# A gated SmoothQuant and mixture-of-experts layer on one core: work moved between VectorE, ScalarE and GpSimd, and the engines' orders rewritten

## The reference

```python
def smooth_quant_linear(x, w):            # x: [T, D], w: [O, D]
    s = sqrt(max(amax_x, 1e-6) / max(amax_w, 1e-6))    # per feature: maxima of |x|, |w| over rows
    xs, ws = x / s, w * s
    x_scale, w_scale = rowmax(|xs|) / 127, rowmax(|ws|) / 127
    return round(xs / x_scale) @ round(ws / w_scale).T * x_scale * w_scale.T

def xattn(x, gu, dw):                     # one batch: gate and up weights, down weights
    gate, up = split(smooth_quant_linear(x, gu))
    return smooth_quant_linear(silu(gate) * up, dw)

def ffn(x):                               # 1024 tokens, 8 experts, room for 128 tokens each
    gates = softmax(x @ w_gate); e = argmax(gates)     # top 1, first come first served
    return gates[e] * (gelu(x @ w1[e]) @ w2[e])        # tokens past an expert's room: 0

x = x + tanh(g_xattn) * xattn(layernorm(x), ctx_gu, ctx_d)
x = x + tanh(g_ffn) * ffn(layernorm(x))
```

## Time and profile before

| | before |
|---|---|
| time of the runs shown | 108.6 us, median of 3 (108.21 to 108.82) |
| profiled execution, device time | 108.64 us |
| its span, first to last instruction | 106.8 us |
| busy share of the span: PE, DVE, ACT, POOL | 90%, 78%, 67%, 55% |
| granted TensorE clock, mean | 0.998 |
| HBM read, written | 20.46 MB, 2.10 MB |

### The profile page before, as it was taken

How to read it: one execution, slowest core, us unless ns; L and a number is a source line. 1 busy time by engine, 2 the same in 40 slices (tenths; PEclk the granted TensorE clock), 3 DMA queues, 4 the chain that set the end, 5 groups by cost and what they waited for, 6 DMA issues and landing times.

```text
span 106.8 us, 2202 instructions
## 1 busy us (share of the span) xinstructions
PE 96.1 (90%) x740; PEld 81.5 (76%) x740; DVE 83.6 (78%) x243; ACT 71.7 (67%) x158; POOL 58.2 (55%) x102
## 2 busy tenths in 40 slices
PE   0999599998799999999999999999999999999940
PEld 0336358877656977889789998999989999899930
DVE  1599999999892999999795299999959669397510
ACT  5012999999899899619842919997849748396000
POOL 6063779898988589967777103452705207051141
PEclk9999999999999999999999999999999999999999
DMA  0999199989962932401586999997999200001011
GB/s 27 278 301 354 56 392 371 372 272 412 302 219 58 333 109 96 167 33 29 134 368 218 396 357 407 352 421 219 403 392 364 72 0 34 15 0 55 0 49 49
DMA packets 14602, 22.66 MB, mean 212 GB/s; under 512 B 1287, under 2 KB 13063, under 8 KB 13568
## 3 DMA queue, kind: packets, MB, share of 16 engines
q1 hardware_dynamic: 13824, 20.46, 55.1%
q0 software_dynamic: 768, 2.07, 5.4%
HBM read 20.46 MB, written 2.10 MB: 211 GB/s over the span
## 4 chain that ended last, share of the span: by engine, by line
PE 59%; DVE 27%; POOL 5%; issue 4%; POOLq 1%; DVEq 0%
PE bk L1425 27%; PE bk L1436 12%; PE bk L1438 6%; PE bk L1244 6%; DVE am L805 4%; DVE x L886 3%; DVE am L758 2%; PE bk L1372 2%; PE bk L1409 2%; DVE wide_a L826 2%; DVE am L752 2%; POOL wide_a L376 1%; POOLq L38 1%; DVE prio L901 1%; DVE ama L853 1%
## 5 line engine op out<-in xcount | busy, mean ns | idle before, releaser
L498 POOL DMA_INDIRECT out<-xrow,sidx x8 | 14.1, 1758 | 31.3 <-DVE xrow L1050 29.8
L1425 PE MATMUL bk<-rows_w,w_sb 128*128 128x128 f32 x192 | 23.1, 276 | 0.1
L1425 PEld LDWEIGHTS bk<-rows_w,w_sb 128*128 128x128 f32 x192 | 22.2, 192 | 0.3 <-DVE rows_w L992 0.2
L1436 PE MATMUL bk<-w2p,hh 128*128 128x512 f32 x56 | 20.7, 408 | 0.1
L1038 DVE TENSOR_TENSOR hl<-bk,hh 128x512 fp32r<-128x512 f32 x16 | 10.8, 686 | 6.8 <-ACT hh L611 6.7
L1438 PE MATMUL bk<-w2p,hl 128*128 128x256 f32 x56 | 15.7, 281 | 0.0
L590 ACT ACTIVATE w2p<-w_sb 128x1024 fp32r<-128x1024 f32 x12 | 12.3, 1054 | 5.0 <-PE bk L1438 5.0
L1244 PE MATMUL bk<-identb,upper 128*128 128x512 bf16 x40 | 12.3, 450 | 2.6 <-POOL upper L311 2.6
L1031 DVE TENSOR_TENSOR w2p<-w_sb,w2p 128x1024 fp32r<-128x1024 f32 x12 | 14.2, 1218 | 0.3
L1436 PEld LDWEIGHTS bk<-w2p,hh 128*128 128x128 f32 x56 | 10.6, 189 | 2.8 <-issue 0.6
L604 ACT ACTIVATE bk<-bk 128x512 f32<-128x512 f32 x16 | 9.4, 585 | 2.0 <-PE bk L1425 2.0
(11 more groups left out here) (177 smaller groups left out, 225.2 us busy)
## 6 DMA issues: line engine op xcount, KB each, us to landing
w_sb<-in_w SPq DMA_DIRECT2D x12, 1024.0 KB, 6.6
x<-in_x SPq DMA_DIRECT2D x4, 256.0 KB, 3.9
cw<-in_ctx_gu SPq DMA_DIRECT2D x4, 256.0 KB, 4.4
cw<-in_w SPq DMA_DIRECT2D x1, 1024.0 KB, 5.7
out<-x SPq DMA_DIRECT2D x4, 256.0 KB, 2.5
x<-in_w SPq DMA_DIRECT2D x1, 1024.0 KB, 4.9
wide_a<-in_w SPq DMA_DIRECT2D x1, 1024.0 KB, 4.9
wide_b<-in_w SPq DMA_DIRECT2D x1, 1024.0 KB, 8.4
```

Source lines behind the costliest of these rows:

```text
L498: nc.gpsimd.indirect_dma_start(out_rows, bass.IndirectOffsetOnAxis(ap=sidx[:, e:e + 1], axis=0), yo[:, e % 2, :], None, bounds_check=last_ ...
L1425: ins = nc.tensor.matmul(HB[e % 2][:, m, n * C:(n + 1) * C], wv[:, k, f:f + P], xgT[:, e % B, k], start=(k == 0), stop=(k == K - 1))
L1436: nc.tensor.matmul(YB[e % 2], hh[:, e % 2, n], w2p[:, e % 2, n].rearrange("p a d -> p (a d)"), start=(n == 0), stop=False)
```

## The change

The arithmetic is the same; two formulas are written with fewer operations, some operations change their engine, and the lists are written in another order.

- `floor_w` goes: the guard is taken inside `product_w` and `ratio1`. `mean_eps` leaves VectorE and becomes a third operation of GpSimd's `row_part`.
- The gate and up weights of batch 3 are scaled by GpSimd (`scale1_w(3)`) instead of ScalarE; `load_w2(3)` and `turn2(3, 1)` wait for that.
- The down weights are scaled by VectorE (`scale_dw`) instead of ScalarE; `turn4` waits for both.
- The second norm's six rows on GpSimd and two on VectorE become four on ScalarE (`norm2(0)`, `norm2(1)`, with a new `shift2` on GpSimd), three on GpSimd and one on VectorE.
- `split_low` and `expert_out` can do part of their range. `split_low(0, 1)` runs in two halves, one of them right behind `add_x(0)`; `expert_out(0, 1)` in four parts, with `slots_turn(1)` in their middle. Two of the fills go.
- ScalarE's `split_high(0, 0)` and `(0, 1)` move ahead to `scale2`, the tanh of the gates to the first `quantise1`. The load of the gelu table stays behind `half_logits`.

```diff
-            sp.wait_ge(scaled1[1], B)
+            sp.wait_ge(scaled1[1], B - 1)
+            sp.wait_ge(scaled_pool, 1)
             load_w2(3)
...
+            def scale1_w(b):
+
+                pool.wait_ge(scale1_ready, b + 1)
+                for k in range(K):
+                    last = nc.gpsimd.tensor_scalar(xs1[:, b, K + k], cw[:, b, k], sc1[:, b, K + k:K + k + 1], 1.0, ALU.mult,
+                                                   ALU.mult)
+                last.then_inc(scaled_pool, 1)
...
                 link(nc.gpsimd.tensor_tensor(std1[:, b], ve1[:, b], rs1[:, b], ALU.mult))
+                nc.gpsimd.tensor_scalar(x[:, b, :, D], nm1[:, b], -1.0, DELTA, ALU.mult, ALU.add)
...
+            def shift2(b):
+
+                pool.wait_ge(rstd2_ready, b + 1)
+                nc.gpsimd.tensor_tensor(sh2[:, b], nm2[:, b], x1[:, b, :, D + L], ALU.mult).then_inc(shift2_ready, 1)
...
-                nc.scalar.activation(aw[:, b, 0], a_sb[:, b], ACT.Identity, scale=sc3[:, b, 0:1])
-                nc.scalar.activation(aw[:, b, 1], dw[:, b], ACT.Identity,
-                                     scale=sc3[:, b, 1:2]).then_inc(scaled2, 1)
+                nc.scalar.activation(aw[:, b, 0], a_sb[:, b], ACT.Identity, scale=sc3[:, b, 0:1]).then_inc(scaled2, 1)
...
+            def norm2(b):
+
+                act.wait_ge(shift2_ready, b + 1)
+                for j in range(J):
+                    last = nc.scalar.activation(xn2[:, b, j], x1[:, b, j, 0:D], ACT.Identity, scale=x1[:, b, j, D + L:H],
+                                                bias=sh2[:, b, j:j + 1])
+                last.then_inc(norm2_act_ready, 1)
...
-                done["product_w", b] = mark(nc.vector.tensor_tensor(pr1[:, b], am1[:, b, 0:K], rw1[:, b], ALU.mult))
+                done["product_w", b] = mark(nc.vector.scalar_tensor_tensor(
+                    out=pr1[:, b], in0=am1[:, b, 0:K], scalar=EPS, in1=rw1[:, b], op0=ALU.max, op1=ALU.mult))
...
-                nc.vector.tensor_tensor(ra1[:, b], pr1[:, b], fl1[:, b], ALU.max).then_inc(ratio1_ready, 1)
+                nc.vector.tensor_scalar(ra1[:, b], pr1[:, b], EPS * EPS, None, ALU.max).then_inc(ratio1_ready, 1)
...
+            def scale_dw(b):
+
+                dve.wait_ge(scale2_ready, b + 1)
+                nc.vector.tensor_scalar(aw[:, b, 1], dw[:, b], sc3[:, b, 1:2], None, ALU.mult).then_inc(scaled_dw, 1)
...
-            def split_low(e, h):
+            def split_low(e, h, first=0, count=4):
...
+                part = slice(4 * h + first, 4 * h + first + count)
...
+                pe.wait_ge(scaled_dw, b + 1)
...
-            def expert_out(e, m):
+            def expert_out(e, m, first=0, count=4):
...
-            fill(2, 0, 2)
             expert_out(0, 0)
+            expert_out(0, 1, 0, 1)
+            expert_out(0, 1, 1, 1)
             slots_turn(1)
-            expert_out(0, 1)
+            expert_out(0, 1, 2, 1)
+            expert_out(0, 1, 3, 1)
```

More of the change, by code:

```diff
@@ L634, in _ @@
             quantise1(0, 1)
+            quantise1(0, 0)
+            tanh_gates()
             scale1(2, 0)
-            quantise1(0, 0)
+            quantise1(1, 1)
             quantise1(1, 0)
-            quantise1(1, 1)
+            move1(0)
+            quantise1(2, 1)
+            scale1(3, 0)
             move_row1(0)
[L640 to L643, removed]
+            move_row1(1)
             quantise1(2, 0)
-            move_row1(1)
+            move1(1)
+            quantise1(3, 1)
             silu(0)
-            quantise1(3, 1)
-            move1(1)
+            quantise1(3, 0)
             move1(2)
-            quantise1(3, 0)
+            silu(1)
             move_row1(2)
-            silu(1)
+            move_row1(3)
+            move1(3)
             silu(2)
             scale2(0)
-            move1(3)
-            move_row1(3)
+            split_high(0, 0)
+            silu(3)
             scale2(1)
-            silu(3)
+            split_high(0, 1)
             quantise2(0)
             scale2(2)
-            tanh_gates()
+            scale2(3)
             quantise2(1)
-            scale2(3)
             move2(0)
-            move2(1)
             quantise2(2)
             quantise2(3)
+            move2(1)
+            move2(2)
             square2(0)
-            move2(2)
             square2(1)
+            square2(2)
             move2(3)
-            split_high(0, 0)
-            square2(2)
+            norm2(0)
+            norm2(1)
             square2(3)
             first_turned()
-            split_high(0, 1)
+            split_high(1, 0)
             half_logits()
@@ L883, in add_x @@
                 dve.wait_ge(row_x_ready, b + 1)
-                dve.wait_ge(dve_c, max(done["mean_eps", b], done["minus_mean", b]))
+                dve.wait_ge(dve_c, done["minus_mean", b])
                 for j in range(J):
@@ L1163, in _ @@
             amax4(3)
-            mean_eps(3)
             guard4(3)
@@ L1204, in _ @@
             hotc_(3)
+            relative_logits()
             first_turned()
+            ovr()
             gather_index()
             scatter_index()
[L1208 removed]
             split_low(0, 0)
[L1210 to L1211 removed]
+            split_low(0, 1, 2, 2)
+            split_low(1, 0)
             hidden_low(0, 0)
@@ L1216, in _ @@
             expert_in(2)
+            expert_in(3)
             softmax()
-            expert_in(3)
+            slot_gates_out()
             hidden_low(1, 0)
-            split_low(1, 0)
+            hidden_low(1, 1)
             split_low(1, 1)
-            slot_gates_out()
-            hidden_low(1, 1)
             expert_add(0)
@@ L1434, in expert_out @@
                     pe.wait_ge(y_ready, e - 1)
-                for n in range(4 * m, 4 * m + 4):
+                for n in range(4 * m + first, 4 * m + first + count):
                     nc.tensor.matmul(YB[e % 2], hh[:, e % 2, n], w2p[:, e % 2, n].rearrange("p a d -> p (a d)"),
@@ L1439, in expert_out @@
                                            start=False, stop=(n == NF - 1))
-                if m == 1:
+                if m == 1 and first + count == 4:
                     ins.then_inc(y_used, 1)
@@ L1498, in _ @@
             fill(1, 1, 6)
+            turn4(2)
             turn5(0)
+            turn4(3)
             fill(2, 1, 3)
-            turn4(2)
+            product2(0)
             turn5(1)
-            turn4(3)
-            product2(0)
+            turn5(2)
             product2(1)
-            turn5(2)
+            product2(2)
+            positions(0)
             fill(3, 1, 1)
             turn5(3)
-            positions(0)
             positions(1)
-            product2(2)
             product2(3)
+            positions(2)
             sort(0)
             sort(1)
-            index(0)
-            positions(2)
             positions(3)
             sort(2)
+            index(0)
             sort(3)
```

217 lines of the change are left out of this document (107 added, 110 removed).

## The result

The changed kernel took 113.79 us (median of 4 runs, 112.44 to 114.07), the kernel before 108.53 us beside it: a ratio of 1.0444, with a 95% interval of 1.0405 to 1.0483. It is slower by 5.3 us, where 108.4 us was forecast and the range ended at 109.3 us. The profiled execution took 113.73 us with a span of 111.8 us, so its span is 5.0 us longer than before.

The account below looks back on a forecast made before the run. TensorE bounds the kernel from 48.05 us, mostly VectorE before. Span 106.8 - 0.04 (earlier start) - 0.15 (after it) = 106.6 us; with 1.84 us around it 108.45 us, forecast 108.4 us, range 107.3 to 109.3 us.

Parts of the forecast that it names:

- ScalarE, GpSimd and VectorE up to add_x(0): Before the residual additions: silu(1) 1.13 us earlier, second act product 1.21 earlier, recip4(1) 0.62 later, add_x(0) 1.29 earlier.
- second rival: VectorE and GpSimd hinder each other, scale_dw at 0.50 us each: H up to 0.9 us later, 109.2 us; chance 0.16.
- VectorE's last stage and H: From add_x(0) to hot0(2) 9.13 us, ending 0.14 us earlier; first hidden product at 48.01 us, not 48.05 us.
- H: Start of the first expert's hidden product on TensorE: 48.05 us in the kernel before, forecast 48.01 us.
- third rival: Batch 3 is late: product2(3) and move2(3) queue behind other work, add_x(3) waits 0.6 us, 109.0 us; chance 0.10.
- After H: 0.15 us earlier: After the first hidden product, slots_turn(1)'s weight load no longer costs matmuls its wait for rows_w: 0.15 us saved.
- TensorE's clock: A fall of the granted clock in one of the new gaps would make the forecast wrong; no size or chance given.
- The table "does not come earlier": On ScalarE the gelu table's 1.28 us load stays behind half_logits, so the wait until the first expert_out stays.
- the expected lead: On VectorE amax3(1) starts 1.21 us earlier, but recip4(1) comes 0.62 us later, 1.30 us of it lost to scale_dw.

Follow-up runs that it names:

- both repairs: Changed kernel with softmax back ahead of expert_in(3) and three fills on TensorE ahead of positions(1): 108.81 us, 1.0006 of the kernel before.
- softmax in front: Changed kernel with one VectorE pair put back, softmax ahead of expert_in(3): 108.93 us, 1.0005 of the kernel before.
- load alone: Changed kernel with only load_w1(3) waiting for the third gather instead of the first: 108.89 us, 1.0015 of the kernel before.
- three fillers: Changed kernel with three fills in TensorE's idle 0.83 us ahead of positions(1): 112.14 us, 1.0309 of the kernel before.

## Why the prediction was wrong, by its own steps

- *ScalarE, GpSimd and VectorE up to add_x(0): right.* Silu(1) 25.25 us (25.35 forecast), amax3(1) 26.58 (26.65), recip4(1) 32.43 (32.60), add_x(0) 35.59 (35.75). Scale_dw took 0.34 to 0.49 us, so the second rival's price was partly paid, and it did not decide. (That rival's sum has a slip: the 0.18 us that it gives for four scale_dw at 0.50 us is the excess of one over 0.325 us; the four make 0.70 us, and its 0.9 us needs them.)
- *VectorE's last stage and H: right in the mechanism, 0.15 to 0.65 us too early.* Hot0(2) at 44.93 us (44.88). With the sorts at full clock H is not at 48.01 us but at 48.16 to 48.36 us in six profiled executions of the new order, and at 48.55 to 48.66 us in four that were already some 0.3 us late at positions(1). In all of these product2(3) waits 0.22 or 0.23 us for move2(3) behind square2: a small form of the third rival.
- *"After H: 0.15 us earlier": the step that failed.* It says that gathers start 0.4 us later against H, "with more than a microsecond in hand". The first gather did start 0.36 us later (0.77 us after H; 0.41 us before). But the third started 1.24 us later (4.78 us after H; 3.54 us before), since the first issue took 2.27 us and not 1.31 us, and the time in hand was that of an order that no longer held: with expert_in(3) ahead of the softmax, the softmax and slot_gates hang on the third gather. I saw the exchange in the new order and gave it no term. Had I asked what the third gather shares its time with, SyncE's load of w1(3), released by the first gather, would have shown. It costs 2.3 us with the clock up (111.1 against 108.9 us), of which the exchange makes 0.9 us with the gathers as early as in the kernel before; moving the load alone takes all of it away, and so does undoing the exchange alone. The other term of this step was right in sign: from H to the first product of hidden(1,0) it takes 7.64 us with both repairs and 7.92 us before, 0.28 us less where 0.15 us was forecast, and that makes up for the later H there. The issues of the kernel before that this rests on are its first and third:

```profile
48.46 1.31 POOL L489 DMA_INDIRECT gr<-out,gidx  x1 [1.11 <-DVE gidx L969]
...
51.59 1.00 POOL L489 DMA_INDIRECT gr<-out,gidx  x1 [0.30 <-issue]
```

- *TensorE's clock: named as what would make the forecast wrong, and not priced.* It fell behind the 0.83 us before positions(1) and behind the idle time before slot_gates, each in some executions; a fall cost 1.3 us by the sorts' rows and 1.6 us by hidden(2)'s. It should have been a rival with a chance of its own; the range ended at 109.3 us.
- *The table "does not come earlier": right*, 50.26 us in the changed kernel. But making it earlier is worth nothing, which the prediction left open.
- *Where the expected lead went.* The 1.2 us that amax3(1) gains are eaten by scale_dw and the reordered reductions, as forecast; they never reach H.

What stays open is what decides, from one execution to the next, whether the clock falls after the same gap: without fillers and without the wait for the gather it was 4 of 22 runs (softmax in front; load alone), with the three fillers and without that wait 3 of 63, in the kernel before none of the 89 timed beside these. So the new order, with its gap, differs in this from the kernel before; that the three fillers lower the count is likely, but so few falls do not show it. Where the clock fell in the runs that were not profiled was not seen.

## What to carry to other kernels

When an order changes, list for every instruction that now stands ahead of others what it waits for, and follow that transfer back to what shares the DMA engines with it and what releases that: a wait that was harmless at the end of a queue is on the path one place earlier. A gap on TensorE is not priced by its length alone: look at what it may do to the granted clock behind it, and give that a chance of its own. And a step made earlier is worth only the distance to what is late next.

## What the runs showed of the hardware

- An indirect DMA's issue on GpSimd that begins while VectorE subtracts from two SBUF operands (split_low) lasts until 0.9 to 1.2 us after that instruction's end: 2.27 us where it began 0.12 us into one, 1.45 us where it began 0.64 us into one, 1.12 us where it began 0.97 us into one. It took 1.31 us where it began 0.27 us ahead of one, and 1.00 us beside a reciprocal, an instruction with one input, that ran on for 0.47 us. The Trainium skill, GPSIMD Engine Reference, section Specifications, says that the two engines share SBUF interfaces and contend when VectorE has two SBUF inputs; the runs agree, and show that who begins first decides. That both inputs must lie in SBUF they do not show: an issue that began 0.21 us before the end of a hidden_low, one of whose operands lies in PSUM, took 1.08 us.
- A gather took 2.9 us from issue to use with no load but the other gathers beside it, and 5.66 us with a 1 MB load started 0.16 us later.
- The same program with the same 0.83 us of idle TensorE kept its clock at 1.00 in one profiled execution and fell to 0.50 for some 3 us in another.
